# Eight-tile transformer block: the quantized rows turned over by a DMA transpose instead of TensorE, context rows dealt to partitions in another order

## What is computed

```
q1 = fake_quant(layernorm(x), x1_scale, x1_zp)      # integers 0..255, minus the zero point, times a scale
q2 = fake_quant(context, x2_scale, x2_zp)
x  = x + q1 @ q2                                    # per batch: [64,1024] @ [1024,1024]
x  = x + attn(layernorm(x))                         # 32 heads of 32, one key/value head, causal, ALiBi
x  = x + ffn(layernorm(x))                          # sign weights, 8 routed input and output scales
```

## Time and profile before

| | |
|---|---|
| median of 3 runs | 459.28 us (459.07 to 462.09) |
| the profiled execution | 458.08 us, span of its instructions 456.3 us |
| mean granted TensorE clock | 0.924 of full speed |
| PE, PEld busy | 382.4 us (84%), 262.2 us (57%) |
| DVE busy | 313.6 us (69%) |
| ACT busy | 264.7 us (58%) |
| POOL busy | 99.9 us (22%) |
| DMA | 90.42 MB, mean 198 GB/s |

### The profile page before, as it was taken

How to read it: one execution, slowest core, us unless ns; L and a number is a source line. 1 busy time by engine, 2 the same in 40 slices (tenths; PEclk the granted TensorE clock), 3 DMA queues, 4 the chain that set the end, 5 groups by cost and what they waited for, 6 DMA issues and landing times.

```text
span 456.3 us, 9695 instructions
## 1 busy us (share of the span) xinstructions
PE 382.4 (84%) x4000; PEld 262.2 (57%) x4000; DVE 313.6 (69%) x584; ACT 264.7 (58%) x314; POOL 99.9 (22%) x112
## 2 busy tenths in 40 slices
PE   0436854996799999999999989998999899889665
PEld 0116734955255965587558745884588458745332
DVE  7698476974748858785878597859885975384331
ACT  4688986664885757575757575756666632242110
POOL 4420010004112312231223122312131212021202
PEclk9966976898599999999999999999999999989759
DMA  8999992599686754675458545854480010001001
GB/s 331 359 411 417 418 404 110 205 382 381 222 287 242 266 188 141 220 289 187 138 205 305 186 139 185 325 185 141 163 330 19 1 47 2 1 1 47 0 1 46
DMA packets 15522, 90.42 MB, mean 198 GB/s; under 512 B 1872, under 2 KB 1872, under 8 KB 7248
## 3 DMA queue, kind: packets, MB, share of 16 engines
q1 hardware_dynamic: 13312, 81.83, 48.4%
q10 hardware_dynamic: 2160, 7.87, 4.7%
HBM read 85.50 MB, written 4.19 MB: 197 GB/s over the span
## 4 chain that ended last, share of the span: by engine, by line
PE 68%; DMA 11%; DVE 10%; ACT 5%; issue 4%; POOL 1%; POOLq 0%; SPq 0%; DVEq 0%; ACTq 0%
DMA ring<-ctx 11%; PE R L1392 10%; PE T L1229 8%; PE R L1184 7%; PE R L1186 7%; PE R L1185 7%; PE R L1262 6%; PE R L1264 5%; PE R L1265 5%; PE C L1210 5%; PE T L1351 4%; ACT b L460 4%; DVE Pr L899 2%; DVE XL L998 1%; PE R L1286 1%
## 5 line engine op out<-in xcount | busy, mean ns | idle before, releaser
L460 ACT ACTIVATE b<-ring,quant,qpar 128x2048 uint8<-128x2048 f32 x64 | 133.1, 2092 | 12.1 <-DMA ring<-ctx 12.0
L1262 PE MATMUL R<-T_hi,Wqkv_hi 128*128 128x128 f16 x512 | 89.4, 221 | 0.0
L1264 PE MATMUL R<-T_lo,Wqkv_hi 128*128 128x128 f16 x512 | 89.3, 221 | 0.0
L1265 PE MATMUL R<-T_hi,Wqkv_lo 128*128 128x128 f16 x512 | 89.2, 221 | 0.0
L1392 PE MATMUL R<-sgn,T_hi 128*128 128x512 fp8e4 x128 | 51.1, 399 | 0.0
L1262 PEld LDWEIGHTS R<-T_hi,Wqkv_hi 128*128 128x128 f16 x512 | 50.8, 99 | 0.4
L1210 PE MATMUL C<-b,aT 128*64 128x512 f16 x256 | 38.5, 429 | 14.8 <-ACT b L460 12.3
L1264 PEld LDWEIGHTS R<-T_lo,Wqkv_hi 128*128 128x128 f16 x512 | 50.6, 99 | 0.2
L1392 PE MATMUL R<-sgn,T_lo 128*128 128x512 fp8e4 x128 | 50.7, 396 | 0.0
L1265 PEld LDWEIGHTS R<-T_hi,Wqkv_lo 128*128 128x128 f16 x512 | 50.6, 99 | 0.0
L1184 PE MATMUL R<-Wo,attT_hi 128*128 128x512 f16 x128 | 48.6, 380 | 0.5 <-DVE attT_lo L930 0.5
(11 more groups left out here) (131 smaller groups left out, 843.5 us busy)
## 6 DMA issues: line engine op xcount, KB each, us to landing
ring<-ctx SPq DMA_DIRECT2D x64, 1024.0 KB, 6.1
ring<-L_attn_Wo SPq DMA_DIRECT2D x4, 1024.0 KB, 7.6
ring<-L_ffn_weight SPq DMA_DIRECT2D x4, 1024.0 KB, 5.0
out<-X ACTq DMA_DIRECT2D x8, 512.0 KB, 2.6
Wo<-L_attn_Wqkv SPq DMA_DIRECT2D x7, 544.0 KB, 16.0
XN<-x ACTq DMA_DIRECT2D x6, 512.0 KB, 4.1
sgn<-L_attn_Wqkv SPq DMA_DIRECT2D x1, 544.0 KB, 19.3
X<-x ACTq DMA_DIRECT2D x1, 512.0 KB, 3.9
```

The costliest lines, as they stand in the source:

```text
L460: e.activation(b8[:, c % BRING, :], ring[:, slot, :], ACT.Identity, scale=qR2, bias=qZ2).then_inc(s_rf[slot], 1)
L1262: e.matmul(dst, hi, rows[0], start=k == 0 and g == 0, stop=False, skip_group_check=True)
L1264: e.matmul(dst, hi, rows[1], start=False, stop=False, skip_group_check=True)
L1265: last = e.matmul(dst, lo, rows[0], start=False, stop=k == KT - 1, skip_group_check=True)
```

## The change

From tile 2 on, SP issues one DMA transpose per tile (`turn_over`), which reads `a16` and writes `aT`, both in SBUF. The 8 TensorE transposes, the PSUM bank and the ACT copy of these 6 tiles are gone; tiles 0 and 1 keep them. A DMA transpose turns over contiguous blocks of 128 columns, so the context rows are dealt to partitions as k*128 + p instead of 8p + k: a piece is now two runs of 4 KB per partition, 512 KB apart. `turn_over(t)` stands on SP's queue after the last piece of tile t (for tile 2 between its pieces 5 and 6), waits for `s_a` and for the last context product of the tile before, and TensorE's `context(t, 0)` and DVE's next `norm0` wait for its landing (`s_aT`).

```
 T_ORDER = [..., ("F", "Tk"), ("M", "rl"),
-           ("N", "T0"), ("M", "rT"), ("M", "is0"), ("M", "is1")]
+           ("M", "rT"), ("M", "is0"), ("M", "is1")]
 T_ORDER_1 = [...,
-             ("M", "rl"), ("N", "T0"), ("M", "rT"), ("M", "is0"), ("M", "is1")]
+             ("M", "rl"), ("M", "rT"), ("M", "is0"), ("M", "is1")]

-ctx_v = context.rearrange("b (p k) n -> b p (k n)", k=KT)
+ctx_v = context.rearrange("b (k p) n -> b p k n", p=P)

 def load_context(t, first, count):
     for c in range(first, first + count):
         pair, b = divmod(c, 2)
-        src = ctx_v[t * 2 + b:t * 2 + b + 1, :, pair * 2 * H:(pair + 1) * 2 * H]
-        load_piece(c % RING, uses(t, c), ring[:, c % RING, :], src.rearrange("o p n -> (o p) n"))
+        src = ctx_v[t * 2 + b:t * 2 + b + 1, :, 2 * pair:2 * pair + 2, :]
+        load_piece(c % RING, uses(t, c), ring[:, c % RING, :].rearrange("p (k n) -> p k n", k=2),
+                   src.rearrange("o p k n -> (o p) k n"))
+
+def turn_over(t):
+    e.wait_ge(s_a, t + 1)
+    at_least(e, s_ctx, t * 4)
+    e.dma_start_transpose(out=aT[:, :, :], in_=a16[:, :]).then_inc(s_aT, 16)

 # SP, first half of a step
-load_context(s.i, 4, 4)
+if s.is_step(2):
+    load_context(2, 4, 2)
+    turn_over(2)
+    load_context(2, 6, 2)
+else:
+    load_context(s.i, 4, 4)
+    if s.i > 2:
+        turn_over(s.i)

 # ACT, second halves of steps 1 to 6
-t0_copy(s)

 # DVE, norm0(t)
-at_least(e, s_T0, t)
+at_least(e, s_T0, min(t, 2))
+at_least(e, s_aT, 16 * (t - 2))

 # TensorE
 def t0(s):
     ...
-    rows = a16[:, :].rearrange("p (c k) -> p k c", k=KT)
     for k in range(KT):
-        last = e.transpose(T[...][:, k * P:(k + 1) * P], rows[:, k, :], ident_h[:, :])
+        last = e.transpose(T[...][:, k * P:(k + 1) * P], a16[:, k * P:(k + 1) * P], ident_h[:, :])
 def context(t, pair, s=None):
     if pair == 0:
-        emptied(s, "T0")
+        if t < 2:
+            emptied(s, "T0")
+        else:
+            e.wait_ge(s_aT, 16 * (t - 1))
 # second halves of steps 1 to 6
-t0(s)
```

More of the change, by code:

```diff
@@ L83 @@
                  ("M", "Ta0"), ("M", "Ta1"), ("F", "Tk"), ("M", "T20"), ("M", "T21"),
-                 ("M", "rl"), ("N", "T0"), ("M", "rT"), ("M", "is0"), ("M", "is1")]
+                 ("M", "rl"), ("M", "rT"), ("M", "is0"), ("M", "is1")]
     @classmethod
     def order(cls, i):
-        return {0: cls.T_ORDER_0, 1: cls.T_ORDER_1}.get(i, cls.T_ORDER)
+        return {-1: cls.T_ORDER_0, 0: cls.T_ORDER_0, 1: cls.T_ORDER_1}.get(i, cls.T_ORDER)
     @staticmethod
@@ L244, in build @@
         s_T0 = sem("s_T0")
+        s_aT = sem("s_aT")
         s_x1 = sem("s_x1sum")
@@ L336, in load_context @@
                     pair, b = divmod(c, 2)
-                    src = ctx_v[t * 2 + b:t * 2 + b + 1, :, pair * 2 * H:(pair + 1) * 2 * H]
-                    load_piece(c % RING, uses(t, c), ring[:, c % RING, :],
-                               src.rearrange("o p n -> (o p) n"))
+                    src = ctx_v[t * 2 + b:t * 2 + b + 1, :, 2 * pair:2 * pair + 2, :]
+                    load_piece(c % RING, uses(t, c),
+                               ring[:, c % RING, :].rearrange("p (k n) -> p k n", k=2),
+                               src.rearrange("o p k n -> (o p) k n"))
[3 more added lines that the diff above has]
+                e.dma_start_transpose(out=aT[:, :, :], in_=a16[:, :]).then_inc(s_aT, 16)
             e.dma_start(quant[:, :], quant_in).then_inc(s_quant, 16)
@@ L1190, in t0 @@
                 e.wait_ge(s_a, s.i + 2)
-                rows = a16[:, :].rearrange("p (c k) -> p k c", k=KT)
                 for k in range(KT):
-                    last = e.transpose(T[:, bank, :].bitcast(F16)[:, k * P:(k + 1) * P],
-                                       rows[:, k, :], ident_h[:, :])
+                    at = slice(k * P, (k + 1) * P)
+                    last = e.transpose(T[:, bank, :].bitcast(F16)[:, at], a16[:, at], ident_h[:, :])
                 last.then_inc(s_T0, 1)
@@ L1516, in second_half @@
                     router(s)
-                if n:
-                    t0(s)
                 if f:
```

## The result

The changed kernel is faster: median 456.30 us of 20 runs against 459.28 us of 20 runs before, ratio 0.9934 with a 95% interval of 0.9915 to 0.9954, so 2.1 to 3.9 us.

What follows compares the result with a forecast made beforehand. Bounds: DMA engines in the first 59 us, then TensorE in repeating steps. Terms -2.7 + 0.9 + 16.1 + 7.6 = +22.0 us on 458.08 gave 480.0, forecast as a median of 481 us; range 457 to 500.

Steps and rivals of the forecast that it cites:

- What L is: Time from `a16` complete to the DMA transpose's landing, taken as 7.2 us, between bounds of 2.6 and 20.1 us.
- the store of 2.6 us: Lower bound for L: a 512 KB store out of SBUF, twice the transpose's bytes, lands 2.6 us after its issue.
- the two terms of 16.1 and 7.6 us: Repeating steps: TensorE waits 3.2 us five times, +16.1 us; a lower clock adds 1.5 us five times, +7.6 us.
- The room of 3.98 us: Step 5, from `a16` complete to first context product without `t0`: 3.98 us, within which a landing makes nothing wait.
- What is lost per us, and the clock: Each us beyond 3.98 is lost on TensorE once per step, five times; a 3.2 us wait adds 1.5 us.
- 0.53 us of TensorE per step: Removing the `t0` transposes from the chain in tiles 3 to 7 saves 0.53 us five times, -2.7 us.
- ACT 0: Removing the copies to `aT`, 1.01 us per tile, gains 0: ACT is not on the chain in repeating steps.
- 4 KB runs +0.9 us: In the DMA-bound first 59 us, context loads in 4 KB runs cost +0.9 us (+0.4 to +1.3).
- piece 6 of tile 1 at 60.3: Sign of slower loads at the start: this piece's first conversion at about 60.3 us instead of 59.36.
- Tile 2 and the queue: Tile 2's transpose, queued behind pieces 4 and 5, costs 0 for L up to about 7; SP's queue costs 0.
- The hidden case: Rival: the landing comes in time (L up to about 4.3 us), 457.5 us, no change; chance 0.22.
- No change by over 1%: Outcome within 1%, from the hidden and small-wait rivals together; chance 0.30.

Runs made afterwards that it cites:

- e5: Changed kernel plus timed DMA transposes and plain copies of growing width after all context products: 1024 columns land after 3.06 us transposed, 2.2 copied.
- e6: Changed kernel with one extra DMA transpose into a spare tile ahead of each true one, not waited for: 462.95 us, ratio 1.0074.
- e7: Changed kernel with one extra DMA transpose into a spare tile ahead of each true one, waited for: 467.00 us, ratio 1.0193.
- e9: Changed kernel with two extra single-block (128-column) DMA transposes ahead of each true one, each waited for: 484.23 us, ratio 1.0526.
- e8: Changed kernel with two extra DMA transposes into a spare tile ahead of each true one, each waited for: 496.56 us, ratio 1.0825.
- e10: Changed kernel with TensorE's transposes and their bank kept beside the DMA transpose, only the ACT copy gone: 457.93 us, ratio 0.9968.
- e2: Kernel before with only the context rows in the new order (4 KB runs), no DMA transpose: 458.58 us, ratio 1.0004.
- e12: Kernel before with an additional ACT copy ahead of each true copy for tiles 2 to 7: 462.75 us, ratio 1.0081.
- e3: Changed kernel with context loads in the old 8 KB runs for every tile, computing another sum from tile 2 on: 455.54 us, ratio 0.9923.
- e4: Changed kernel with the old 8 KB runs for tiles 0 and 1 only: 456.42 us, ratio 0.9950.
- e1: The changed kernel itself, run again on the same chip as other experiments: 455.90 us, ratio 0.9932.
- e11: Changed kernel with tile 2's transpose after pieces 6 and 7 on SP's queue: 463.75 us, ratio 1.0085.

## Why the prediction was wrong, point by point

- **What L is: the step that failed.** The lower end of the two bounds, the store of 2.6 us, was nearly the truth (3.1). I left it for the neighbourhood of 1 MB loads because short pieces "cost more than the small size gives back". They cost 0.9 us over a copy of the same bytes (e5). The landings of 7.6 and 20.1 us are times of queued or four times larger transfers; the store was the row with a transfer of like size, on idle engines, out of SBUF. With L = 3.1 in the sum, the two terms of 16.1 and 7.6 us vanish, and 457.5 us stands.
- **The room of 3.98 us: right.** The first product still comes 3.99 us after the rows, and from there on lateness is paid in full (e6, e7).
- **What is lost per us, and the clock: right at the L assumed.** At that L the sum holds: e9, with L of 7.6 to 9.0, has steps of 50.8 to 51.4 us where the forecast for 7.2 was 50.3, and 484 us where it was 481. That the totals lie so close is partly luck: TensorE also waits 5.95 us for tile 2 there, which the sum had at 0 for L up to about 7. The clock's loss of 1.5 us is there behind every wait from 3.6 us on (e8, e9), absent behind five waits of 2.1 to 2.4 us (e7), and present behind one of 2.19 us (e6). So near 2 us the wait's length alone doesn't tell.
- **0.53 us of TensorE per step: right**, measured 0.51. Doing the work again beside the DMA transpose takes the step back to 46.08 us (e10); 0.07 of the 0.51 us are the contiguous reading (e2), which the sum had not named.
- **ACT 0: right in sign, thin in margin.** The copy was 0.15 us from being felt (e12).
- **4 KB runs +0.9 us: not confirmed, and probably too high.** The 0.06 us per piece are there, but neither e2, e3 nor e4 tells a difference, and the gain of 2.1 to 3.9 us leaves little room for it beside the 2.6 us of the steps. The sign that I had named, piece 6 of tile 1 at 60.3, did not come (59.45, and 59.84 in e1). How much the runs cost, if anything, stays open.
- **Tile 2 and the queue: right for the landing.** A wait of 0.37 us inside a later one; and the price of the other order is as large as thought (e11). The later return of the clock behind tile 2, 0.9 us in the profiled pair, was in no term.
- **The chances.** The hidden case with 0.22 came true in mechanism; the measured 3.0 us (2.1 to 3.9) lie beyond its 1.8 us, and hold the 2.7 us that are left of it without the 0.9 us for the 4 KB runs. No change by over 1% had 0.30, and that it was: -0.66%.

No kernel here beats the changed one. e3 and e4 are within its interval.

## What to carry to other kernels

Between a producer and the engine that needs its result turned over, measure the room in the trace first: a DMA transpose of 128 x 1024 two-byte elements needs 3.1 us on idle DMA engines (4.9 in one case of 35), and with 4 us of room it is a nearly free way to take 8 transposes off a full TensorE. The gain is only what TensorE did (0.5 us per tile), the loss when it is late is every microsecond, in every step, and from some 2 us of waiting on it can be a lower clock on top. To price an operation that the trace doesn't show, take the row that is like it in bytes, source and load of the queues, not one in the middle of the bounds.

## What the runs showed of the hardware

A DMA transpose on idle engines occupies SP for 1.13 to 1.23 us at 128 to 1024 columns, where a load of the context holds it for 0.33 us (8 KB runs) or 0.37 (4 KB runs), and for 4.82 us at 4096 columns. Its landing is nearly flat up to 512 columns (2.25 to 2.46 us) and doubles from 1024 to 2048 columns (3.06 to 5.96 us). Two of them issued back to back hinder each other: the second lands 3.2 to 4.9 us after its issue. In an otherwise full stretch TensorE kept its full clock through five waits of 2.1 to 2.4 us (e7), lost it after one of 2.19 us (e6), and lost it in or behind every wait from 3.6 us on (e8, e9).
